# A graph attention layer on one core: spacing the gathers of its edge stage by the matmuls, and a shorter warm-up

## The reference, cut to what matters

```python
h = jnp.maximum(_layernorm(x), 0.0)                       # [50000, 256]
Q, K, V = h @ Wq, h @ Wk, h @ Wv                          # 8 heads of 32
scores = jnp.einsum('ehd,ehd->eh', Q[dst], K[src]) * SCALE
w = softmax of scores over the edges of one destination
out = zeros.at[dst].add(V[src] * w) @ Wo_w + Wo_b
out = _layernorm(h + out, ln1_g, ln1_b)
out = _layernorm(out + gelu(out @ ffn_w1 + ffn_b1) @ ffn_w2 + ffn_b2, ln2_g, ln2_b)
return x + out
```

## Time and profile before

| | us |
|---|---|
| median of 3 runs | 1763.69 (1762.94 to 1768.16) |
| profiled execution, its own time | 1771.17 |
| its span | 1769.3 |
| PE busy | 1642.7 (93%) |
| DVE busy | 1512.9 (86%) |
| ACT busy | 1320.0 (75%) |
| POOL busy | 1270.5 (72%) |
| score stage, last transpose of head sums (L449) | 401.5 |

### The profile page before, as it was taken

How to read it: one execution, slowest core, us unless ns; L and a number is a source line. 1 busy time by engine, 2 the same in 40 slices (tenths; PEclk the granted TensorE clock), 3 DMA queues, 4 the chain that set the end, 5 groups by cost and what they waited for, 6 DMA issues and landing times.

```text
span 1769.3 us, 31077 instructions
## 1 busy us (share of the span) xinstructions
PE 1642.7 (93%) x10389; PEld 1472.7 (83%) x10389; DVE 1512.9 (86%) x4615; ACT 1320.0 (75%) x2419; POOL 1270.5 (72%) x1281
## 2 busy tenths in 40 slices
PE   2878888799888999999999999999999999999997
PEld 2767777687666899999999999999999999999997
DVE  1566666778773899999999999999999999999997
ACT  1465556565444888888888888888888888888884
POOL 7364545505666788888888888888888888888883
PEclk7798889999988999999999999999999999999999
DMA  5487637713425577777777777777777777777761
GB/s 173 142 311 269 239 131 274 288 37 127 133 100 125 123 171 179 176 170 177 177 171 176 175 174 176 175 175 172 176 176 174 174 178 172 175 178 172 174 138 66
DMA packets 95280, 303.91 MB, mean 172 GB/s; under 512 B 16236, under 2 KB 21834, under 8 KB 95120
## 3 DMA queue, kind: packets, MB, share of 16 engines
q0 software_dynamic: 42336, 138.54, 38.9%
q1 hardware_dynamic: 52784, 163.38, 26.5%
HBM read 134.61 MB, written 118.53 MB: 143 GB/s over the span
## 4 chain that ended last, share of the span: by engine, by line
PE 84%; issue 6%; DVE 4%; ACT 3%; another core or an unknown queue 2%; DMA 0%; DVEq 0%; SPq 0%; POOLq 0%; POOL 0%; ACTq 0%
PE banks L962 32%; PE banks L951 30%; PE banks L384 8%; PE banks L937 5%; PE banks L406 3%; PE banks L904 2%; PE banks L392 2%; ACT a_hs L335 2%; DVE c_total L811 1%; PE banks L923 1%; PE banks L376 1%; DVE c_msg L799 1%; ACT a_htd_hi L302 1%; PE banks L893 0%
## 5 line engine op out<-in xcount | busy, mean ns | idle before, releaser
L962 PE MATMUL banks<-d_w_hi,d_act_hi 128*128 128x256 f32 x1564 | 457.4, 292 | 0.0
L962 PE MATMUL banks<-d_w_lo,d_act_hi 128*128 128x256 f32 x1564 | 442.0, 283 | 0.0
L962 PE MATMUL banks<-d_w_hi,d_act_lo 128*128 128x256 f32 x1564 | 441.6, 282 | 0.0
L1159 ACT ACTIVATE vt<-vt,d_zx_nmr,d_zx_rstd 128x256 f32<-128x256 f32 x391 | 222.8, 594 | 141.6 <-POOL d_zx_nmr L1278 141.6
L951 PE MATMUL banks<-d_zt_hi,d_w_hi 128*128 128x512 f32 (+1 forms) x784 | 306.8, 391 | 2.2 <-DVE d_zt_lo L1044 2.2
L951 PE MATMUL banks<-d_zt_lo,d_w_hi 128*128 128x512 f32 (+1 forms) x784 | 306.4, 391 | 0.0
L951 PE MATMUL banks<-d_zt_hi,d_w_lo 128*128 128x512 f32 (+1 forms) x784 | 305.4, 390 | 0.0
L962 PEld LDWEIGHTS banks<-d_w_hi,d_act_lo 128*128 128x128 f32 x1564 | 298.9, 191 | 0.0
L962 PEld LDWEIGHTS banks<-d_w_hi,d_act_hi 128*128 128x128 f32 x1564 | 298.5, 191 | 0.0
L962 PEld LDWEIGHTS banks<-d_w_lo,d_act_hi 128*128 128x128 f32 x1564 | 297.9, 190 | 0.0
L1260 POOL TENSOR_TENSOR vt<-vt,d_g_row 128x1024 f32<-128x1024 f32 x98 | 289.3, 2952 | 2.9 <-ACT vt L1159 2.9
(11 more groups left out here) (167 smaller groups left out, 3629.4 us busy)
## 6 DMA issues: line engine op xcount, KB each, us to landing
agg_scratch<-vt SPq DMA_DIRECT2D x100, 512.0 KB
vt<-in_x SPq DMA_DIRECT2D x97, 512.0 KB
vt<-agg_scratch POOLq DMA_DIRECT2D x97, 512.0 KB, 5.5
vt<-vt POOLq DMA_DIRECT2D x97, 512.0 KB, 7.5
out<-vt SPq DMA_DIRECT2D x97, 512.0 KB, 2.9
a_xd<-in_x,a_idx POOLq DMA_INDIRECT x98
a_xs<-in_x,a_idx POOLq DMA_INDIRECT x98
score_scratch<-a_score SPq DMA_DIRECT2D x98, 4.0 KB
```

The source lines that it names most:

```text
L962: ins = nc.tensor.matmul(Y[s % 2][:, j, :], a[:, c, j * P:(j + 1) * P], w[:, c, :], start=False, stop=(c == KF - 1 and w is w2_lo), skip_g ...
L1159: ins = nc.scalar.activation(zn[gz % 2][:, j, :], z[gz % ZR][:, j, :], ACT.Identity, bias=zx_nmr[:, at % NR, 0, j:j + 1], scale=zx_rstd[:, ...
```

## The change

Four edits, all in the score stage. The warming products go from 70 to 30. POOL's gathers get three waits: from group 4 on, the first gather of group g waits for the first half of V of step g - 4; the first gather of group 1's side 1 waits for the transposes of group 0's side 0; the first gather of group 2 waits for the first half of Q of group 0. And DVE's order changes in steps -1 and 0, so that statistics stand behind the work that the new waits depend on.

```diff
-    WARM, IDLE = 70, 18
+    WARM, IDLE = 30, 18
...
                     if g >= XG and j == 0:
                         pool.wait_ge(h_done[side], g + 1 - XG)
+                    if g >= XG + 1 and n == 0:
+                        pool.wait_ge(v_done, KD * (g - XG - 1) + 1)
+                    if g == 1 and n == GT:
+                        pool.wait_ge(t_done[0], 1)
+                    if g == 2 and n == 0:
+                        pool.wait_ge(q_done, 1)
...
                 elif s == -1:
                     low_part(0, 0)
+                    low_part(0, 1)
                     statistics(1, (1,))
-                    low_part(0, 1)
                     inverse_root(1)
+                elif s == 0:
+                    products(0)
+                    low_part(1, 0)
+                    head_sums(0)
                     statistics(2, (0,))
+                    low_part(1, 1)
+                    statistics(2, (1,))
+                    inverse_root(2)
+                    statistics(3, (0,))
                 elif s < AHEAD:
```

## The result

The change made the kernel slower: **1786.81 us** (median of 5 runs, 1784.85 to 1794.67) against 1763.69 (5 runs of the kernel before on the same chip, 1758.46 to 1768.16), a ratio of 1.0144 with a 95% interval of 1.0108 to 1.018. I had forecast 1730, with a range of 1685 to 1758. The profiled execution after took 1784.85 us, 13.7 more than the profiled one before.

A forecast was written before the change was run, and what follows sets the result against it. Long unbroken runs of gathers were taken to slow the issue of other engines' instructions and so bound the score stage. Opening 11.8 plus steady steps 22 made 34 us off, forecast 1730 against the median 1763.69, range 1685 to 1758.

The forecast's parts named there:

- rival 5: Slow issue has nothing to do with gathers: first transposes stay at 48.86, steps at 14.65 us, time 1764; chance 0.06.
- (a): Opening, warming products 70 to 30: PE reaches its transposes with 30 products spent; price 1 us for a lower clock.
- (b): Opening, group 1's source gathers behind the first transposes: step 0's source transposes at about 42 instead of 63.96, 22 us earlier.
- Part (c): Opening, groups 2 to 4: 24 contiguous gathers delay step 1; ten of 22 us given back, 11.8 kept.
- Part (d): Steady score steps gated at half of V: runs of eight, steps 13.5 instead of 14.65 us, 22 us gained over nineteen.
- recovery 1.5: Term of the steady step: PE is quick again 1.5 us after the last gather of a run.
- what is left: Term of the steady step: other transposes and half of V after recovery, 2.4 us, less 0.3 done while crawling.
- Part (e): The wait on POOL itself costs nothing; without cover, up to 1 to 2 us in steps 0 and 1.
- Part (f): DVE's new order in steps -1 and 0: same instructions, 1.4 us statistics each, hidden by the opening's delay.
- Rival 4: Slower: ACT's copy of the source side (L302) waits for each run's end; steps 16.7 us, 1791; chance 0.10.
- Rival 2: Score stage: runs of eight never starve anyone; gain 74 us, 1690, or 1672 with the opening's run harmless; chance 0.17.
- rival 3: Score stage: stalls only move, steps stay at 14.65 us and only the opening's gain remains, 1752; chance 0.17.

The follow-up runs named there:

- pauses: Changed kernel plus four GpSimd fills after every four gathers from group 2 on, a 2.56 us pause: 1748.36 us, ratio 0.9906 (starving chip); 1730.23, ratio 1.0493 (free).
- fours: Changed kernel, source side's four gathers from group 4 on also waiting for all of Q of step g - 3: 1739.08 us (starving chip), 1655.29 (free).
- the gates of fours in the old opening: Kernel before plus the wait on half of V and the source-side wait on Q; opening unchanged: 1648.98 us, ratio 1.0, on a free chip.

## Why the prediction was wrong, point by point

**The mechanism held in part.** Runs of gathers do hold up the other engines, and rival 5 (1764, nothing to do with gathers) is out: on starving chips, cutting the runs with pauses or fours brought the time 38 and 48 us below the change's 1786.81. But I had put all of it down to the issue of instructions. ACT's stalls shown here (4.67, 5.74 and 8.98 us, and the one of the earlier trace rows) are waits for a count of PE's that comes late. The crawl is something else: the warming products of the earlier trace rows wait for no count and give none, and after 54 of them they come one by one all the same.

**Parts (a) and (b)** were right. PE idles until 20.87, the first transposes take 1.97 us at the lower clock, and step 0's source transposes came at 42.98 (forecast 42).

**Part (c)** was too dark. I had 24 gathers in a row from 30.5 to 60.7. They are 16 from 29.14 to 48.85, then eight from 52.65. I had the gate met before its turn, and by PE's timeline it was (the six products of the first half of V ran from 38.41 to 41.3), yet POOL stood still for 3.81 us. ACT's copy of the same half of V also waited, 8.98 us:

```profile
51.91 1.07 ACT L324 COPY vt<-banks 128x512 f32<-128x512 f32 x2 [8.98 <-remote]
```

Both waited for the same semaphore, `v_done`, and its counts, due at 41.32 and 42.81, are recorded at 51.88 and 51.96, 3 us after the run of 16 ends. So POOL, too, waited for a late count of PE's. Step 1's source transposes stand at 67.77 instead of 72, and 16 us were gained, not 11.8.

**Part (d) is the step that failed.** It had 13.5 us a step; it is 16.1. One step from gate to gate, that is from the count of half of V at 145.38 to the end of the next half at 162.00, gives term by term:
- release 0.1 us: 0.8 (POOL starts at 146.14).
- the run 9.8: 9.7, right.
- recovery 1.5: 2.2 (155.85 to about 158.1).
- what is left, 2.4 less 0.3 of work done while crawling: 3.9 to the end of the next half of V, with 2.8 us of it at the clock level of 1.2 GHz. I had costed the transposes and V after the crawl at the higher clock, though the earlier trace rows had 1.91 us for eight transposes after an idle stretch and the earlier trace rows 1.10 in a busy one. In the step above they take 1.91.

That is 0.8 + 9.7 + 2.2 + 3.9 = 16.6 for this step, against 13.5. The supply was too large as well: I took 9.0 us from the run of 162.44 in the kernel before, where PE had done 62 products; the changed kernel's eights are dry at 54, 7.2 us into the run. So PE reaches three quarters of K and not its end. That adds little to the sum. In the 4.7 us from there to the recovery it does almost nothing (1.65 us of work), but this is five of K's last six products, and one is left for afterwards.

The deeper error is in the shape of the sum. In the kernel before (its cycle of the earlier trace rows) the twelve (eight and four, 1.2 us apart) costs one long crawl in three steps, a four costs none, and the eight costs ACT 3.1 us. With a gate at V nearly every step has an eight and nearly every step has its crawl, its refill and its stretch at the lower clock. I counted gathers in a run and not the number of runs that outlast the supply.

**Part (e)**: the wait cost nothing by itself; on a free chip the steps with it are 10.9 us. The prediction's 1 to 2 us for late gathers did show, but in the opening: DVE waits 1.96 us for group 1 on the free chip, and is 4.6 us later than in the kernel before. **Part (f)** wasn't measured apart from the waits. On the free chip the late gathers account for 4.6 of the 5.6 us, so little is left for it.

**Rivals.** Rival 4 had the right sign and nearly the right step (16.7 us, 1791), by another instruction: in the changed kernel its copy waits 0.23 us, and PE's K products are what starves. The stall that it named exists, 5.74 us of it in the kernel with fours. Rival 2 (eights never starve) and rival 3 (stalls only move) gave 1690 and 1752. Rival 2 would have been right in its premise on a free chip, where even 128 gathers in a row starve no one; but there is nothing to gain there.

The Trainium skill, page Runtime: NRT & Kernel Launch, section Instruction fetch mechanics, says that an engine's instructions are streamed in by a queue of its own and that the cost is mostly hidden; it gives TensorE room for 2048 of them. The free chips agree with the first. On the starving ones PE is dry after 51 to 57 products in the changed kernel's eights, each with a weight load, so some hundred instructions; if it is the fetching that stops, the store was never near full. The trace speaks against the fetching. It keeps the packets of the instruction queues, and one queue brings 16 KB at a time, 82 packets in all. I take it to be PE's, whose 20698 products and weight loads would make some 250 instructions a packet (an estimate). One of these packets came in the run from 146.14, at 148.42, and took 0.96 us, no more than outside of runs; PE was dry 4 us and some thirty products after it. In the run from 129.60 none came, and PE lasted as long: 52 products, against 53 by the same count. What does stop stays open: the record shows late counts and late products, and not what holds both up.

## What to carry to other kernels

Before regrouping work that disturbs others, count the disturbances that outlast their reserve, and give each its whole price: the crawl, the recovery after it and the slower clock behind it. Short bursts with gaps (fours 2.56 us apart) cost the score stage nothing of the stall; twice the length cost 5 us a step against an undisturbed one (16.1 against 10.9). And measure on more than one chip: here the change is worth +23 us on one kind, +7 on another, and the fours -24 on one and +6 on the other, so a version should be kept only if it loses on neither; the gates of fours in the old opening cost nothing on a free chip, but were not tried on a starving one. And where an engine waits though its input is done, compare the end of the instruction that it waits for with the time at which its count is recorded.

## What the runs showed of the hardware that was not expected

- Chips of one type differ: the kernel before took 1763 to 1765 us (medians) on the chip of the comparison and on the two of the experiments that starve, and 1649 to 1650 on three others. In the two traces, 1769.3 and 1647.9 us long, about 103 of the 121 us between them are in the score stage (last source transposes at 394.1 and 291.5); the rest of the span is 1375 us on the one kind and 1356 on the other. Why the chips differ stays open.
- On the starving chips runs of POOL's indirect DMAs hold the others up. Plain ones of half the size, in steady runs of 8.2 us and once for 41 us without a break, and with more traffic (310 against 234 GB/s), don't: 1671.76 against 1786.81 for the change.
- What is held up is PE's counts as well as its next products: on a starving chip counts came up to 10.6 us after the product (due at 41.32, recorded at 51.88), and engines with their input done stood still for them. On the free chips, and with plain DMAs on a starving one, all of PE's counts from 9 to 300 us come within 0.02 us (220 of 220 in the changed kernel, 224 of 224 with the plain ones).
- An indirect gather of 128 rows takes POOL 1.25 to 1.26 us from start to start on every chip traced, a plain DMA of 128 rows 0.53 (4.3 us for eight), one of 64 rows 0.51 (8.2 for sixteen).
